# One core of Trainium2: the hand-written instruction order of a decoder layer with routed experts is written anew on four engines, and its last expert is split differently

## The reference: what is computed

```
x = layernorm(x + attn(x))          # 16 heads of width 8; q, k = relu(.) + 1e-6; causal linear attention
                                    # out = sum_{j<=i} (q_i.k_j) v_j / sum_{j<=i} q_i.k_j, then out_w
x = layernorm(x + xattn(x, ctx))    # 16 heads of width 8; queries x, keys and values ctx;
                                    # softmax over |i-j| <= 64, then W_proj
x = layernorm(x + ffn(x))           # 8 experts, top-1 of a softmax gate; at most 641 tokens per expert,
                                    # in order of token; h = gelu(t @ W1 + b1); y = h @ W2 + b2; times gate
```

## Time and profile before

| | |
|---|---|
| median of 3 runs | 431.02 us (429.87 to 433.3) |
| the profiled execution, its own time | 431.97 us |
| its span, first to last instruction | 430.2 us |
| PE busy, share of the span | 401.2 us, 93% |
| PEld busy | 298.2 us, 69% |
| DVE busy | 331.8 us, 77% |
| ACT busy | 267.2 us, 62% |
| POOL busy | 252.3 us, 59% |
| mean granted clock of TensorE | 0.989 |

### The profile page before, as it was taken

How to read it: one execution, slowest core, us unless ns; L and a number is a source line. 1 busy time by engine, 2 the same in 40 slices (tenths; PEclk the granted TensorE clock), 3 DMA queues, 4 the chain that set the end, 5 groups by cost and what they waited for, 6 DMA issues and landing times.

```text
span 430.2 us, 19219 instructions
## 1 busy us (share of the span) xinstructions
PE 401.2 (93%) x7097; PEld 298.2 (69%) x7097; DVE 331.8 (77%) x1640; ACT 267.2 (62%) x603; POOL 252.3 (59%) x372
## 2 busy tenths in 40 slices
PE   6999999999999999999999999998888999999960
PEld 5657676777677677777677767776676788888850
DVE  6367688888788888788888898888876487887772
ACT  4755767777777777777777777865546434444420
POOL 5253454566666676666566866666545057677653
PEclk9999999999999999999999999999999999999995
DMA  4910000101101011110111122010021333343100
GB/s 112 317 38 17 15 16 15 28 28 47 29 26 29 28 34 39 36 29 26 28 34 29 39 64 79 21 28 15 17 59 35 102 101 118 112 134 114 32 26 16
DMA packets 25859, 22.74 MB, mean 53 GB/s; under 512 B 3623, under 2 KB 21090, under 8 KB 25766
## 3 DMA queue, kind: packets, MB, share of 16 engines
q1 hardware_dynamic: 23430, 17.30, 13.6%
q0 software_dynamic: 2336, 4.20, 3.1%
HBM read 12.46 MB, written 9.58 MB: 51 GB/s over the span
## 4 chain that ended last, share of the span: by engine, by line
PE 74%; ACT 8%; DVE 8%; issue 5%; POOL 1%; DMA 1%; POOLq 0%; SPq 0%; DVEq 0%; ACTq 0%
PE banks L772 14%; PE banks L722 13%; PE banks L714 8%; PE banks L1222 8%; ACT arena L1508 8%; PE banks L734 7%; PE banks L707 6%; PE banks L784 4%; PE banks L851 2%; PE banks L752 2%; PE banks L800 1%; PE banks L1202 1%; PE banks L753 1%; PE banks L754 1%; PE banks L823 1%
## 5 line engine op out<-in xcount | busy, mean ns | idle before, releaser
L1681 DVE TENSOR_REDUCE mx<-banks 128x8 f32<-128x1024 f32 x64 | 75.6, 1219 | 33.7 <-PE banks L722 33.6
L1247 ACT ACTIVATE arena<-banks 128x1024 f32<-128x1024 f32 x64 | 62.3, 1022 | 31.7 <-PE banks L722 31.7
L772 PEld LDWEIGHTS banks<-arena,V 128*32 128x32 f32 x2048 | 53.1, 109 | 29.9 <-ACT arena L1277 23.4
L1277 ACT ACTIVATE arena<-banks 128x1024 f32<-128x1024 f32 x64 | 62.2, 1021 | 16.7 <-PE banks L714 16.5
L772 PE MATMUL banks<-arena,V 128*32 128x128 f32 x2048 | 67.2, 275 | 0.3 <-ACT arena L1277 0.2
L1508 ACT ACTIVATE arena<-banks,b1T 128x321 f32<-128x321 f32 x64 | 33.8, 529 | 42.1 <-PE banks L1202 41.5
L641 POOL DMA_INDIRECT out_x<-ot,idx x40 | 40.2, 1006 | 23.1 <-DVE ot L2331 14.7
L482 POOL TENSOR_TENSOR rs<-ve,minus_half 128x2 f32<-128x2 f32 x32 | 23.2, 725 | 52.1 <-DVE ve L1669 52.0
L498 POOL DMA_INDIRECT expert_in<-x,sidx x32 | 35.1, 1097 | 14.1 <-DVE x L1755 6.0
L459 POOL TENSOR_TENSOR QE<-qT,head_mask 128x512 f32<-128x512 f32 x32 | 33.1, 1034 | 16.4 <-DVE qT L1592 16.2
L1265 ACT ACTIVATE CE<-banks,head_mask 128x128 f32<-128x128 f32 x128 | 36.6, 371 | 9.7 <-PE banks L707 9.5
(11 more groups left out here) (207 smaller groups left out, 967.6 us busy)
## 6 DMA issues: line engine op xcount, KB each, us to landing
w_sb<-in_L_ffn_W SPq DMA_DIRECT2D x16, 256.0 KB, 3.1
EB<-expert_in SPq DMA_DIRECT2D x9, 325.0 KB, 4.0
expert_in<-zeros SPq DMA_DIRECT2D x10, 266.5 KB, 3.3
X<-in_x SPq DMA_DIRECT2D x32, 64.0 KB, 1.8
C<-in_ctx SPq DMA_DIRECT2D x32, 64.0 KB, 2.0
out_x<-fb SPq DMA_DIRECT2D x32, 64.0 KB, 1.6
out_x<-ot,idx POOLq DMA_INDIRECT x40, 2.2
b2b<-in_L_ffn_b SPq DMA_DIRECT2D x1, 512.0 KB
```

What stands on the lines that cost most here:

```text
L772: mm = pe.matmul(bank(name)[VW * s:VW * (s + 1), half * P:(half + 1) * P], V[:, h, :], scored[:, h // NA, h % NA, :], start=q == 0, stop=q ...
L1247: nc.scalar.activation(A1[b % 2][:, 2 * half:2 * half + 2].rearrange("p j a t -> p j (a t)"), pair("s1", half), ACT.Relu).then_inc(s1_out[ ...
L1277: nc.scalar.activation(P2[b % 2][:, 2 * half:2 * half + 2].rearrange("p j a t -> p j (a t)"), pair("s2t", half), ACT.Exp, scale=SCALE).the ...
L1681: v.tensor_reduce(mx[b % 2][:, 8 * half:8 * half + 8].rearrange("p (j a) -> p j a", a=NA), pair("s2", half).rearrange("p j (a t) -> p j a ...
```

## The change

**Order.** All four step lists are replaced. In the loop over n the steps keep their distance in sequences, except `cT` and `CE`, which come two sequences later than before. On TensorE `t2` and `cT` now stand ahead of `mxT`, and `y2T` behind `t1`. On ACT `lexp` stands between `CE` and `p1`, and `y2Te` behind `fb`. On DVE `mxs` stands ahead of `res2` and `y1Te`, `lg3` to `lg5` all stand ahead of `mx1`, `rk2` stands between `mx1` and `mx0`, and `ve2` stands behind `k`, `v` and `fbs`. On POOL `QE` stands ahead of `x2`, and the scatter is one sequence earlier. In the last sequences ACT does `p0` ahead of `p1`, DVE does `rk4(26)` ahead of the maxima of sequence 31, and POOL does `scatter(26)` ahead of `pow2(29)`; `rk(31)` stands ahead of two late products.

**Banks.** `y1T`, `xT`, `o2`, `y2T` and `x2T` move.

**Prologue.** TensorE gets identity products in three more places; the turning of the other weights comes ahead of the first `qkv`; the first `cT` comes later.

**Last expert.** Groups [0], [1, 2], [3], [4] for [0], [1, 2], [3, 4]. The odd rows of experts 0 to 6 are added ahead of the last `second_layer`, the last one behind its first tile, and they are scattered second instead of last. ACT applies scale and shift (Identity with two per-row operands) in place of DVE, for which `inverse` also computes a shift; the epsilon goes into ACT's Sqrt as its bias.

```diff
-JOBS = [("y1T", 2, (6,)), ("lg", 8, (7,)), ("xT", 0, (3,)), ("o2", 6, (0,)), ("o1", 2, (1,)), ("t2", 4, (6,)),
+JOBS = [("y1T", 2, (0,)), ("lg", 8, (7,)), ("xT", 0, (6,)), ("o2", 6, (6,)), ("o1", 2, (1,)), ("t2", 4, (6,)),
...
-        ("x1T", 2, (0,)), ("pv1", 1, (5,)), ("s2", 2, (2, 3, 6, 7)), ("y2T", 5, (5,)), ("t1", 1, (7,)),
-        ("x2T", 7, (6,)), ("pv2", 3, (4,)), ("s1", 0, (1, 2, 4, 5))]
+        ("x1T", 2, (0,)), ("pv1", 1, (5,)), ("s2", 2, (2, 3, 6, 7)), ("y2T", 5, (0,)), ("t1", 1, (7,)),
+        ("x2T", 7, (5,)), ("pv2", 3, (4,)), ("s1", 0, (1, 2, 4, 5))]
...
-    SETUP_BANK, WEIGHTS_BANK = 6, 0
+    SETUP_BANK, WEIGHTS_BANK = 1, 0
...
@@ POOL, loop
-            for n in range(6, 26):
+            for n in range(5, 26):
                 at(op_x1b, n - 3)
-                at(op_scatter, n - 10)
+                at(op_scatter, n - 9)
                 at(op_pow2, n - 6)
-                at(op_v2, n - 1)
+                at(op_QE, n)
+                at(op_v2, n - 2)
                 at(op_x2, n - 6)
-                at(op_QE, n)
                 at(op_pow1, n - 2)
                 at(op_x1, n - 2)
                 at(op_xb, n - 1)
...
@@ PE, prologue
             op_xT(0)
+            busy(3)
             pe.wait_ge(setup_done, 1)
+            turn_other_weights()
             op_qkv(0)
+            busy(4)
             op_xT(1)
-            turn_other_weights()
-            op_cT(0)
+            op_xT(2)
+            busy(3)
             op_s1(0)
             op_qkv(1)
-            op_cT(1)
             still_busy(3, 4)
             op_pv1(0)
...
@@ PE, loop
-            for n in range(7, 27):
-                at(op_xT, n - 1)
-                at(op_s1, n - 2)
-                at(op_rk, n - 9)
-                at(op_o2, n - 7)
-                at(op_y1T, n - 3)
-                at(op_qkv, n - 1)
-                at(op_lg, n - 8)
-                at(op_x1T, n - 4)
-                at(op_o1, n - 3)
+            for n in range(6, 27):
+                at(op_t2, n - 6)
+                at(op_cT, n - 4)
                 at(op_mxT, n - 5)
-                at(op_t2, n - 6)
-                at(op_cT, n - 2)
                 at(op_s2t, n - 5)
                 at(op_s2, n - 4)
                 at(op_pv1, n - 2)
                 at(op_pv2, n - 5)
-                at(op_y2T, n - 6)
                 at(op_x2T, n - 7)
                 at(op_t1, n - 2)
+                at(op_y2T, n - 6)
+                at(op_xT, n)
+                at(op_s1, n - 1)
+                at(op_rk, n - 8)
+                at(op_o2, n - 6)
+                at(op_y1T, n - 2)
+                at(op_qkv, n)
+                at(op_lg, n - 7)
+                at(op_x1T, n - 3)
+                at(op_o1, n - 2)
...
             early_rows()
-            late_rows(B - 3, 1)
             op_rk(B - 1)
             late_rows(B - 3, 0)
+            late_rows(B - 3, 1)
...
+                    if e == E - 1 and k == 1:
+                        pe.wait_ge(y_done, e * JT + 1)
+                        odd_rows(e, True).then_inc(rest_full, 1)
...
+                if e == E - 1:
+                    pe.wait_ge(t_done, 2 * E)
+                    pe.wait_ge(y_done, (E - 2) * JT + 1)
+                    for before in range(E - 1):
+                        odd_rows(before, False)
                 second_layer(e)
-            pe.wait_ge(t_done, 2 * E)
-            pe.wait_ge(y_done, (E - 1) * JT + 1)
-            for e in range(E):
-                mm = odd_rows(e, e == E - 1)
-            mm.then_inc(rest_full, 1)
...
@@ ACT, loop
+            for n in range(4, 25):
+                at(op_s1e0, n)
+                at(op_s1e1, n)
+                at(op_mxTe, n - 3)
+                at(op_CE, n - 2)
+                at(op_lexp, n - 7)
+                at(op_p1, n - 3)
+                at(op_p0, n - 3)
+                at(op_yx1, n)
+                at(op_yx2, n - 3)
+                at(op_x2Te, n - 5)
+                at(op_fb, n - 7)
+                at(op_y2Te, n - 4)
...
@@ ACT, last expert
+            root(first)
+            root_rest()
+            scaled(first, 1)
+            scaled_rest(2)
+            root(first + 1)
+            scaled(first + 1, 3)
+            root(first + 2)
+            scaled(first + 2, 4)
+            root(first + 3)
+            scaled(first + 3, 5)
...
@@ DVE, loop (new)
+            for n in range(8, 29):
                 at(op_x1Te, n - 6)
                 at(op_res1, n - 5)
+                at(op_mv2, n - 9)
+                at(op_rec2, n - 8)
+                at(op_q, n - 3)
+                at(op_n2, n - 8)
+                at(op_k, n - 3)
+                at(op_v, n - 3)
+                at(op_fbs, n - 10)
                 at(op_lg2, n - 10)
+                at(op_ve2, n - 9)
                 at(op_lg3, n - 10)
                 at(op_st1, n - 5)
+                at(op_lg4, n - 10)
+                at(op_lg5, n - 10)
                 at(op_mx1, n - 6)
+                at(op_rk2, n - 11)
                 at(op_mx0, n - 6)
                 at(op_mxh, n - 6)
+                at(op_rk3, n - 11)
                 at(op_den1, n - 4)
                 at(op_mv1, n - 5)
                 at(op_rec1, n - 4)
                 at(op_ve1, n - 5)
                 at(op_n1, n - 4)
                 at(op_xTe, n - 2)
+                at(op_rk4, n - 11)
+                at(op_rk1, n - 10)
+                at(op_mxs, n - 6)
+                at(op_res2, n - 8)
+                at(op_y1Te, n - 4)
+                at(op_st2, n - 8)
+                at(op_lg1, n - 9)
...
@@ DVE, last expert
+            mark = tile(0)
+            spread_of(last, 0, mark)
+            rest_summed(rest_mark)
+            rooted(first, 1)
+            mark = tile(1)
+            rest_rooted(2)
+            spread_of(last, 1, mark)
+            mark = tile(2)
+            spread_of(last, 2, mark)
+            mark = tile(3)
+            rooted(first + 1, 3)
+            spread_of(last, 3, mark)
+            mark = tile(4)
+            spread_of(last, 4, mark)
+            rooted(first + 2, 4)
+            rooted(first + 3, 5)
```

More of the change, by code:

```diff
@@ L229, in decoder @@
         y_bank = max_bank + act_bank
-        GROUPS = [(e, tiles) for e in range(E) for tiles in ([[0, 1], [2, 3, 4]] if e < E - 1 else [[0], [1, 2], [3, 4]])]
+        GROUPS = [(e, tiles) for e in range(E) for tiles in ([[0, 1], [2, 3, 4]] if e < E - 1 else [[0], [1, 2], [3], [4]])]
         r3 = ring("r3", 2, [P, ET, D])
@@ L660, in _ @@
                 scatter(2 * e + 1, [0, 1, 2])
-            first, second, third = range(2 * E - 2, 2 * E + 1)
+            first, second, third, fourth = range(2 * E - 2, 2 * E + 2)
             scatter(first, [0])
+            scatter_rest()
             scatter(second, [0, 1])
-            scatter(third, [0, 1])
-            scatter_rest()
+            scatter(third, [0])
+            scatter(fourth, [0])
         @block.tensor
@@ L1512, in _, with root, root_rest, scaled @@
             nc.scalar.activation(warm[:], ones[:, 0:1], ACT.Sqrt)
-            for n in range(2 * E - 2, 2 * E + 1):
-                e, tiles = GROUPS[n]
-                group = slice(tiles[0], tiles[-1] + 1)
+            last, first = (E - 1) % 2, 2 * E - 2
+            def root(n):
+                c0, c1 = GROUPS[n][1][0], GROUPS[n][1][-1] + 1
                 act.wait_ge(var3_ready, n + 1)
-                nc.scalar.activation(sd3[:, group], ve3[e % 2][:, group], ACT.Sqrt).then_inc(root_ready, 1)
-            act.wait_ge(var_rest, 1)
-            nc.scalar.activation(sdr[:], ver[:], ACT.Sqrt).then_inc(root_ready, 1)
+                nc.scalar.activation(sd3[:, c0:c1], mv3[last][:, c0:c1, 1], ACT.Sqrt, bias=eps[:]).then_inc(root_ready, 1)
+            def root_rest():
+                act.wait_ge(var_rest, 1)
+                nc.scalar.activation(sdr[:], mvr[:, 1:2], ACT.Sqrt, bias=eps[0:E, :]).then_inc(root_ready, 1)
+            def scaled(n, ready):
+                act.wait_ge(scale_ready, ready)
+                before = [len(GROUPS[m][1]) for m in range(n % 4, n, 4)]
+                act.wait_ge(out_done[n % 4], 16 * sum(before))
+                for t, c in enumerate(GROUPS[n][1]):
+                    nc.scalar.activation(ot[n % 4][:, t, :], r3[last][:, c, :], ACT.Identity, scale=rs3[last][:, c:c + 1],
+                                         bias=shift3[:, c:c + 1]).then_inc(ot_ready, 1)
+            def scaled_rest(ready):
+                act.wait_ge(scale_ready, ready)
+                nc.scalar.activation(otr[:], r3r[:], ACT.Identity, scale=rsr[:], bias=shiftr[:]).then_inc(ot_rest, 1)
+            root(first)
[8 more added lines that the diff above has]
+            scaled(first + 3, 5)
         @block.vector
@@ L2296, in spread_of @@
                 own.wait(mark)
-                own.mark(v.bn_aggr(mv3[e % 2][:, c, :], st3[:, c % 2, :]))
-                for of, tiles in GROUPS:
-                    if of == e and tiles[-1] == c:
-                        own.wait()
```

(23 more changed lines are left out.)

862 lines of the change are left out of this document (383 added, 479 removed).

## The result

| | before | after |
|---|---|---|
| median | 431.42 us, four executions (429.87 to 433.3) | 424.19 us, four executions (423.19 to 427.51) |
| profiled execution | 431.97 us | 425.13 us |
| its span | 430.2 us | 423.4 us |
| mean granted clock | 0.989 | 0.981 |

The ratio is 0.984 with a 95% interval of 0.9811 to 0.9869: faster by 1.6%, 7 us.

A forecast was written before the change was run, and what follows sets the result against it. TensorE was taken to bound the loop, with a wait for the maxima each period. Loop -4.6, prologue -0.5, loop end -1.5, last expert +0.75: -5.85 us, 426.1 from the profiled 431.97; forecast 425.5, range 419.5 to 431.5.

The forecast's parts named there:

- The wait at `mxT` goes: Loop, TensorE: the wait for the maxima, about 0.38 us a period with what comes with it, disappears; margin near 1 us.
- the 0.2 us a period for `lexp`: Loop, ACT: lexp between CE and p1 makes p1 late and gives back 0.2 us a period (0 to 0.35).
- The 8.95: Loop: period in us seen where mxs is ready, taken as the base to which 0.2 was added.
- the spared switch of types: Loop, TensorE: the new order spares one f32 to bf16 switch and back (0.14 us); period 9.15 becomes 9.1.
- GpSimd and `x2`: Loop: QE ahead of x2 leaves TensorE's x2 load a cover of about zero to 0.3 us; nothing charged.
- The new banks: Loop: o2 waits for xTe and x1T for y1Te, ready 0.1 to 0.3 us ahead; cost nothing if DVE is punctual.
- Rival (b): Loop: oh or cand, 0.2 us later, meets QE and waits up to 1.3 us; +3.8 us, 434.5 in all; chance 0.08.
- Prologue: Before the loop: later qkv(0) +1.0, clock -1.7 or identity products +1.9, cT and CE -1; sum -0.5 us (-2.5 to +1.5).
- End of the loop: Last sequences: earlier scatter(26), scatter(27) and x2(31), against three CE on ACT; -1.5 us, range -3 to +1.
- Last expert: End of kernel: early odd rows delay every tile and POOL's scatters stand 1.25 us apart; +0.75 us, range -1 to +1.5.
- Rival (d): Last expert, ACT: alternating Sqrt and Identity reloads tables, seven switches of 1.28 us, +9 us, 434; chance 0.02.
- Rival (a): Loop: the wait moves to p1, x2T or o2's bank; period 9.2 to 9.3, loop -1 to -2 us, 429; chance 0.20.

The follow-up runs named there:

- b_mxs: The kernel before with one edit: in VectorE's loop mxs stands ahead of res2, y1Te, rk4, rk2 and st2; 425.02 us, ratio 0.9847.
- a_lexp: The changed kernel with lexp behind p0 instead of between CE and p1 in ACT's loop; 425.18 us, ratio 0.9832 to the kernel before.
- b_both: The kernel before with two edits: t2 and cT ahead of mxT, and mxs ahead of res2; 424.81 us, ratio 0.9833.
- b_t2cT: The kernel before with one edit: in TensorE's loop t2 and cT stand ahead of mxT; 429.14 us, ratio 0.9929.

## Why the prediction was right

**The total** was near (426.1 forecast for the profiled execution, 425.13 measured; 425.5 and 424.19 by medians), partly because terms that were off cancelled.

- *The wait at `mxT` goes:* right, by the chain's 0.06 us and by b_mxs, and it is nearly the whole result. My margin of 1 us is about right too: `mxs` starts 1.53 us ahead of its use for 0.41.
- *The term that was mis-sized:* the 0.2 us a period for `lexp` on the path to `p1`. It was 0, as a_lexp shows: undisturbed, the loop takes 8.88 us with `lexp` on either side. The floor that I had built on was lower too. The 8.95 came from the written-out last sequences, whose order is another; the old loop without the wait takes 8.90, in b_mxs as in b_both, so the 0.05 for the spared switch of types isn't seen between these two. Over all 24 periods the changed kernel took 9.01, since 0.13 us of disturbances that I hadn't forecast filled up part of what the 0.2 left; 24 times the 0.09 below my 9.1 are the 2 us by which the loop did better.
- *GpSimd and `x2`:* charged at nothing, and nearly right: 0.13 us in six of 24 periods. The wait at `x2T`, which I had named as a sign of being wrong, is there in those periods, because a pause of VectorE that I didn't know of uses up the cover. *The new banks:* nothing, and right; the weight loads behind `x1Te` wait there and are hidden.
- *Rival (b)* was placed rightly and given too firm a margin. I had it at 0.2 us; the same loop in another program loses it in every other period, from a pause of 0.28 us in VectorE's instruction stream that no semaphore explains.
- *Prologue:* `qkv(0)` at 7.8 was right (7.83). The -0.5 was +0.21 in the profiled execution. The other executions show a gain of 0.6 at s2t(0), and with the 0.71 behind it 1.3 in all. That the identity products bring the higher level earlier was right, by `s1(0)` in all fourteen traces; that the level can fall again, as in the changed kernel from 8 to 11 us, I hadn't thought of. The 1.9 us that I charged for the ten products otherwise has no working: ten of 0.4 are 4.
- *End of the loop:* -1.5 was too much: it is -0.66, of which 0.40 lie ahead of s2t(31). Against s2t(31) scatter(27) came 0.28 us earlier, not 1.3, and `x2(31)` 0.2, not 1.0. Moving scatter(26) did save 1.31 us between `pow2(29)` and `x2(29)`, but `pow2(29)` starts 0.73 us behind s2t(31) for 0.22 before, behind a later `ve2`, and scatter(27) now waits 0.71 us behind `x2(29)` for 0.17; why, I didn't trace. From there on all is as before: `early_rows` waits for the landing, and GpSimd stands at scatter(28) until its DMA lands. (The timeline's bracket names ACT's `fb`, for which scatter(28) doesn't wait; the chain names the DMA.) In the changed kernel, the second row from the chain, the others from the timeline:

```profile
309.63 1.09 POOL L501 DMA_INDIRECT expert_in<-x,sidx  x1 [0.71 <-POOL x L492]
...
312.48 2.71 DMA odd_row<-expert_in
...
316.05 1.09 POOL L501 DMA_INDIRECT expert_in<-x,sidx  x1 [2.56 <-ACT fb L1292]
...
318.01 0.80 POOL L492 TENSOR_SCALAR x<-r,mv,rs 128x128 f32<-128x128 f32 x1
```

- *Last expert:* the sign and the mechanism (GpSimd's spacing behind a delayed second layer) were right, 0.47 for 0.75; the second layer starts 0.62 us later, for my 0.75. The sign that I had named for it was badly put: counted from the start of that second layer the last scatter is 0.15 us earlier (13.17 for 13.32), since the delay lies ahead of that start.
- *Rival (d)* is out: the run has three table loads, as before, and Sqrt alternates with Identity in the last expert with none between. *Rival (a)* as I had it, with the gain lost, appeared nowhere; a part of it is in b_t2cT (`cT`'s product) and at `x2T`. Its "-1 to -2" doesn't follow from periods of 9.2 to 9.3, which give -2.2 to +0.2.

Open: why a drop of the clock behind the loop meets some executions and not others; why VectorE pauses with no semaphore in every second period, and at a place that differs between kernels with the same loop; and the single periods in which TensorE is slower by itself (masks at 0.40 us for 0.22, `pv` at 2.21 to 2.38 for 2.06).

## What to carry to other kernels

When TensorE's chain holds one short wait per period, look first for what stands needlessly ahead of the releasing instruction on the other engine: one VectorE step moved past five gave as much as a new order of four engines. A walk that adds durations of overlapping small instructions overcharges (1.71 for 1.58 us here); take start-to-start times. Before a difference of 1 to 3 us is put down to an edit, compare the same stretch in several profiled executions, with its granted clock.

## What the runs showed of the hardware

- Of one and the same prologue, executions had TensorE at 1.2 or at 2.4 GHz from 8 to 11 us: 1.9 us at s2t(0) between the two ends.
- Identity products that fill TensorE's first pauses bring the 2.4 GHz level earlier: `s1(0)` took 1.08 to 1.14 us in nine executions with them and 2.03 to 2.09 in five without.
- A VectorE instruction of 128 x 8 elements that began together with a GpSimd tensor_tensor of 1.03 us ended with it (1.06 us); one that began 0.12 us ahead took its usual 0.23; a tensor_reduce out of PSUM ran beside it undisturbed. One of 128 x 16 that began 0.02 us behind a tensor_tensor of 0.46 us took 0.47, and 0.08 us ahead 0.16.
- VectorE's instruction stream paused by 0.23 to 0.29 us with no semaphore, in every second loop period from 9 to 21. Around an unchanged loop the place moved with the rest of the program, from ahead of `ve2` to ahead of `cand`, and the period was 9.05 us in place of 8.97.
